# GpSimd instead of ScalarE issues the loads of the staged weights and the stores of their halves

## The reference

```python
h = _layernorm(x, axis=-1) * (1 + ca) + sa
x = x + ga * _L0_attn_ref(h, Wqkv, bqkv, Wout, bout)      # 16 heads, causal softmax
h = _layernorm(x, axis=-1) * (1 + cb) + sb
# feed-forward, E, H, I = (8, 256, 512), TOP_K = 1
logits = x @ router_w.T
top_vals, top_idx = jax.lax.top_k(logits, TOP_K)
...
routed = jnp.einsum('etf,efh->eth', up * jax.nn.silu(gate), down_proj)
shared = jax.nn.silu(x @ shared_gate_w) * (x @ shared_up_w) @ shared_down_w
x = x + gb * (shared + routed_sum)
```

## Time and profile before

| | us |
|---|---|
| median of 3 runs | 463.87 |
| lowest and highest | 460.45, 464.77 |
| the profiled execution | 461.35 |
| its span, first to last instruction | 459.6 |
| busy in it: PE, DVE, ACT, POOL | 398.2, 313.6, 227.7, 212.8 |

### The profile page before, as it was taken

The page is one execution under the profiler, slowest core; times in us unless marked ns, Lnnn a source line. Parts: engine busy times, 40 slices in busy tenths (PEclk is TensorE's granted clock), DMA queues, the critical chain, the costliest instruction groups (busy, mean ns, idle before and its releaser), DMA issues.

```text
span 459.6 us, 8603 instructions
## 1 busy us (share of the span) xinstructions
PE 398.2 (87%) x3009; PEld 224.8 (49%) x3009; DVE 313.6 (68%) x635; ACT 227.7 (50%) x408; POOL 212.8 (46%) x251
## 2 busy tenths in 40 slices
PE   3789986598989899878989799999879999999991
PEld 3244542243554356434435264575555666666660
DVE  7678597268999898799968864879553434444441
ACT  2445556288584867547865746263213333232320
POOL 2395954343336963177354653101601555555342
PEclk9999999699999999999999999999999999999997
DMA  8547489359692578734357004992700444333210
GB/s 270 165 117 159 166 218 230 118 186 276 243 252 83 170 206 265 210 118 138 96 172 232 1 20 166 397 350 77 227 24 25 84 87 82 83 72 82 26 21 0
DMA packets 46192, 67.96 MB, mean 148 GB/s; under 512 B 5380, under 2 KB 33668, under 8 KB 46152
## 3 DMA queue, kind: packets, MB, share of 16 engines
q1 hardware_dynamic: 31064, 36.74, 27.4%
q10 hardware_dynamic: 9936, 22.55, 15.1%
q0 software_dynamic: 5152, 8.14, 9.0%
HBM read 43.14 MB, written 25.18 MB: 149 GB/s over the span
## 4 chain that ended last, share of the span: by engine, by line
PE 51%; DVE 18%; DMA 9%; ACT 7%; issue 5%; SPq 4%; POOL 3%; ACTq 1%; DVEq 0%; POOLq 0%
PE bank L1513 35%; DVE mx L1146 4%; DMA qk_d<-W 4%; DMA ng_d<-negm 4%; PE bank L1669 3%; PE bank L1653 3%; PE bank L1894 2%; SPq L541 2%; DVE rowg L1247 2%; ACT W L896 2%; PE bank L1624 2%; PE bank L1601 1%; DVE W L1247 1%; DVE x_sb L1191 1%; PE bank L1528 1%
## 5 line engine op out<-in xcount | busy, mean ns | idle before, releaser
L896 ACT ACTIVATE W<-bank 128x512 f32<-128x512 f32 (+1 forms) x176 | 93.7, 562 | 61.6 <-PE bank L1653 43.5
L1146 DVE TENSOR_REDUCE mx<-bank 128x1 f32<-128x384 f32 (+3 forms) x176 | 104.9, 632 | 27.4 <-PE bank L1626 24.0
L1513 PE MATMUL bank<-W 128*128 128x256 f16 (+2 forms) x756 | 103.9, 289 | 5.3 <-DVE x_sb L1191 1.7
L1513 PEld LDWEIGHTS bank<-W 128*128 128x128 f16 x756 | 72.7, 99 | 38.1 <-issue 8.5
L768 POOL TENSOR_SCALAR_AFFINE_SELECT W<-W 128x512 f32<-128x512 f32 x64 | 47.8, 748 | 83.9 <-ACT W L896 83.9
L1653 PE MATMUL bank<-W 128*128 128x512 f16 (+3 forms) x256 | 63.3, 304 | 18.9 <-ACT W L896 9.7
L1513 PE MATMUL bank<-W,h2T 128*128 x276 | 67.3, 380 | 2.8 <-DVE W L1262 2.0
L839 POOL DMA_INDIRECT out<-h2T,sidx x23 | 36.3, 1578 | 67.5 <-DVE h2T L1483 67.1
L1624 PE MATMUL bank<-W 126*128 126x128 f16 (+3 forms) x208 | 52.5, 304 | 5.6 <-DVE mx L1146 4.2
L1669 PE MATMUL bank<-W 128*32 128x128 f32 (+3 forms) x512 | 48.6, 454 | 0.8 <-POOL W L768 0.8
L1653 PEld LDWEIGHTS bank<-W 128*128 128x128 f16 x256 | 21.3, 97 | 55.6 <-ACT W L896 29.2
(11 more groups left out here) (173 smaller groups left out, 558.8 us busy)
## 6 DMA issues: line engine op xcount, KB each, us to landing
w_d<-rowg ACTq DMA_DIRECT2D x18, 512.0 KB, 3.7
W<-w_d SPq DMA_DIRECT2D x18, 512.0 KB, 7.9
stage<-in_gup ACTq DMA_DIRECT2D x14, 512.0 KB
qk_d<-W SPq DMA_DIRECT2D x48, 128.0 KB
W<-qk_d SPq DMA_DIRECT2D x32, 192.0 KB, 5.1
stage<-in_down ACTq DMA_DIRECT2D x7, 512.0 KB
x_sb<-in_x SPq DMA_DIRECT2D x4, 512.0 KB, 9.5
h_d<-gbb SPq DMA_DIRECT2D x4, 512.0 KB, 4.6
```

Of the source, the lines that this page charges most:

```text
L896: a.activation(PT[j][:, i:i + m, :], t_bank(N)[:, 0:m * w].rearrange("p (i n) -> p i n", i=m), ACT.Exp).then_inc(s_exp, 1)
L1146: v.tensor_reduce(mx_v[:, b % 2, hp0 // 4, par, i:i + m, t], s_bank(N)[:, 0:m * w].rearrange("p (i n) -> p i n", i=m), AX.X, ALU.max).then ...
L1513: i = t_.matmul(outp, l, r, start=(n == 0), stop=(n == len(prods) - 1), **kw)
```

## The change: what it does

`move_halves` leaves ScalarE's stream and enters GpSimd's, at the end of the same step. GpSimd waits for the low half, issues the store, then the load of unit k + 3. The loads that GpSimd issues count on semaphores of their own (`s_pld`); ScalarE's `split_high` waits for those from unit 3 on.

```diff
@@ -388,6 +388,7 @@
         s_eld = [sem(f"s_eld{r}") for r in range(3)]
+        s_pld = [sem(f"s_pld{r}") for r in range(3)]
@@ -497,7 +498,7 @@
             e, u = unit_list[unit(k)]
-            dst, s = staged(k), s_eld[k % 3]
+            dst, s = staged(k), s_eld[k] if k < 3 else s_pld[k % 3]
@@ -774,6 +775,13 @@
+            def move_halves(k):
+                po.wait_ge(*low_done(k))
+                if k < BOUNCED:
+                    g.dma_start(w_d[k], ob[k % 2]).then_inc(s_bw[k % 2], 16)
+                if k + 3 < NU:
+                    unit_in(g, k + 3)
@@ -814,6 +822,9 @@
+                    moved = splits_at(BU * b + n - MOVES)
+                    if moved is not None:
+                        move_halves(moved)
@@ -933,7 +944,7 @@
             def split_high(k):
-                ac.wait_ge(s_eld[k % 3], 32 * (k // 3 + 1))
+                ac.wait_ge(*((s_eld[k], 32) if k < 3 else (s_pld[k % 3], 32 * (k // 3))))
@@ -944,13 +955,6 @@
-            def move_halves(k):
-                ac.wait_ge(*low_done(k))
-                if k < BOUNCED:
-                    ac.dma_start(w_d[k], ob[k % 2]).then_inc(s_bw[k % 2], 16)
-                if k + 3 < NU:
-                    unit_in(ac, k + 3)
@@ -1019,9 +1023,6 @@
-                    moved = splits_at(BU * b + n - MOVES)
-                    if moved is not None:
-                        move_halves(moved)
```

## The result

| | before | changed |
|---|---|---|
| median, us (executions) | 462.16 (4) | 471.77 (4) |
| lowest and highest | 458.15, 464.77 | 470.07, 472.93 |
| the profiled execution, its span | 461.35, 459.6 | 470.88, 469.1 |

The ratio is 1.0244, 95% interval 1.0198 to 1.0289. The change is slower: by 9.6 us between the medians, by about 11 us by the ratio, and by 9.5 us between the two profiled executions. The forecast was 468.4, range 460.0 to 476.0.

What follows compares the result with a forecast made beforehand. No engine was taken as the bound for long: TensorE, VectorE, ScalarE and GpSimd walk in step through the attention loop. -2.5 + 4.9 + 3.4 = +5.8 us on the mean of 462.6 gave 468.4 us, range 460.0 to 476.0.

Steps and rivals of the forecast that it cites:

- The sum: Whole kernel: ScalarE's gain and GpSimd's two late places give +5.8 us; the moved transfers themselves were priced at 0.
- place 1: Sequence 1, ahead of the last `modulate2`: four transfers of units 10 and 11 make GpSimd late for TensorE, +4.9 us.
- three signs: Wrong if new GpSimd rows short, down units' rows 3 times others, or TensorE's `h2_turn` waits under 2 us both places.
- Part 2: GpSimd's price per transfer, taken from gathers: 1.27 us (range 0.4 to 4.3), 56 us for 44, mostly covered by waits.
- Part 3: Sequence 1, second norm: four transfers at 1.27 us, 5.08 less 0.14 us to spare, cost +4.9 us.
- Part 4: Sequence 2, second norm: three transfers delay `rstd`, two more stand behind the first `modulate2`; TensorE waits, +3.4 us.
- Place 2: Sequence 2, about 200 to 216 us: five transfers make GpSimd's mask and `modulate2` late for TensorE, +3.4 us.
- Part 1: ScalarE's issues on the chain: stops near 171 (0.78 us) and 187 us (1.71) vanish, -2.5 us; near 207 nothing.
- rival 2: Attention loop: engines walk in step and absorb late work, so the end does not move (464.3 or 462.0 us); chance 0.25.
- Rival 1: GpSimd hides issues of under about 0.3 us each and ScalarE is set free: faster, 457.7 us; chance 0.08.
- Rival 3: Down-unit loads of 512 pieces cost GpSimd 4.3 us instead of 1.27, one at each place: 474.5 us; chance 0.17.
- Rival 4: VectorE's norm scalings hold up GpSimd's nine transfers at both places, 0.5 us each, 4.4 us more: 472.8 us; chance 0.08.

Runs made afterwards that it cites:

- 2: Against the kernel before: GpSimd issues the transfers from unit 8 on, ScalarE those of units 0 to 7; ratio 1.0129, median 467.08 us.
- 7: Against the changed kernel: moves of units 3 to 6 one step earlier in GpSimd's stream; ratio to the kernel before 1.0193.
- 9: Against the changed kernel: in sequence 0 moves of units 3 to 6 earlier and ahead of `qk_low`; ratio to the kernel before 1.0115, median 464.94 us.
- 10: Against the kernel before: GpSimd issues the moves from unit 8 on except units 10 and 11, ScalarE the rest; ratio 1.0018.
- 12: Against the changed kernel: units 3 to 6 issued early, ahead of `qk_low`, and ScalarE issues units 10 and 11; ratio to before 1.0010, median 461.78 us.
- 8: Against the kernel before: GpSimd issues only the moves of units 13 and 15, ScalarE the rest; ratio 0.9976, median 459.64 us.

## Why the prediction was right or wrong

**Right:** slower by over 1% had 0.54, and 471.77 lies in the range. **But half of the loss is another one than I named.** The sum had -2.5 + 4.9 + 3.4 = +5.8; the runs show relay +5.9, place 1 +4.8, everything else +0.5. **By two of its own three signs the prediction was wrong:** the new rows are short (0.56 to 0.60 us and back to back, not 0.96 and 0.30 apart), and TensorE's waits for `modulate2` before `h2_turn` are 0.7 us in both places. That the total lies in the range is in part luck, since a term left at nothing and a price twice too high made up for each other.

**The step that failed** is in the sum: "The transfers themselves are the same bytes to the same places, issued 0 to 3 us later ... : 0". I had looked at who waits for the moved transfers (nobody for 6 steps) and not at who shares the DMA engines with them. The earlier trace rows stood first in the argument: TensorE waits 7.8 us for `W<-ng_d`. (That piece ends at 85 us, at the relay one sequence earlier; at the one near 112 us, where the changed kernel waits 7.0, it was 0.2 us before.) A chain that runs over transfers at a DMA share of 0.9 to 1.0 is the one place where a shift of 1 MB by 2 us must be priced. I used those rows only to say that gains ahead of them count for nothing; in the changed kernel a loss there counted in full.

**Part 2, the price of a transfer, was mis-sized:** 1.27 us from the gathers, measured 0.56 to 0.60, and 0.79 for 512 pieces. GpSimd's busy time rose by 27 us (239.6 against 212.8), not by 42. The nearest row was not near: a gather is indirect, and a plain transfer is half its price. With the measured prices Part 3 gives 2.6 - 0.14 = +2.5 us. Part 4 gives 0 ahead of `rstd`, then 0.60 + 0.79 - 0.91 = +0.5 us for the two transfers ahead of the mask, which had 0.91 us of idle time.

**Place 1 was the right place and mechanism.** Predicted +4.9; the profiles show +3.1 to +4.3, the ratios 4.8. The transfers are 2.6 us of it, not 5.1, and the low half that now meets GpSimd ahead of the last `modulate2` is 1.0 us. TensorE's longest wait of 2.3 us is for the stretched mask ahead of it, not for `modulate2`. The sum was near because a price twice too high stood in for a stretch that I had not seen there.

**Place 2 is far smaller than predicted (+3.4):** `rstd` is not late, and GpSimd loses 0.6 us on the two transfers behind it. The exponentials fall back 2.2 us between steps 22 and 38, but they had gained 2.8 just before. Over steps 12 to 38 the net is -0.5 us in kernels 2, 7, 9, 10, 12 and the changed one, and -1.1 us in 8, where GpSimd issues unit 15's move but not unit 16's: 0.6 us for place 2, from profiles alone.

**Part 1:** the stop at 187 us is real, 2.0 us by step 16 in kernels 8, 12 and the changed one (predicted 1.7). The one at 171 us gave nothing (predicted 0.8). In kernel 8 half of the first is given back by step 22, as rival 2 said of engines that walk in step.

**The rivals.** Rival 1 needed about 0.3 us an issue to be faster, and set the point where gain and loss cancel at 0.6. The measured price is at that point, yet the kernel is far slower, since place 1 costs more than the transfers' own time and the relay was in neither. Rival 3 falls: 0.79 us, not 4.3. The Trainium skill, "DMA: Bandwidth & Descriptors" (section "Anatomy of one DMA — SWDGE (gpsimd) path"), which let many descriptors pass before the increment, agrees with that. Rival 4 put the cost on the wrong instructions. The 18 stores take 0.55 to 0.84 us, median 0.58, so the transfers are held up by 0.3 us at most. Of the nine in the two places three lie beside a scaling (0.65, 0.55 and 0.63 us, no longer than elsewhere), and none of the 44 beside a low half, so what that would do to a transfer was not seen. But the mask and the `modulate2` behind them lost 1.0 us to VectorE's low half, once at place 1 and not nine times 0.5. The low half reads two buffers, `stage` and `rowg`, and by the Trainium skill, "SBUF — State Buffer" (section "Who interferes with whom"), a VectorE instruction with two SBUF inputs contends with a GpSimd instruction that reads SBUF. The 1.62 us against 0.63 agree in direction; no run here shows that this is the cause. The row of 1.58 us at 205.77 that the prediction showed also lies beside a low half, the one at 205.27, for 1.0 us, and beside a scaling for only 0.2. The Trainium skill, "DMA: Bandwidth & Descriptors" (section "SWDGE vs HWDGE vs iDMA"), says that the transfer engines round-robin between queues of the two kinds. One could take that to mean that a load of 8 KB passes a backlog of another queue soon; the section gives no time for it. The table shows 1.8 us against 4.8 us, with GpSimd's backlog as with ScalarE's: the measured number decides, and a backlog costs it 3 us.

**What stays open:** whether the stretch beside the low half comes from shared ports (no kernel took the low half away), why the `qk_d` hop is 2 us longer behind a later unit 3 (how its packets stand in the queues was not seen), how often the kernel before loses the race, and why holding unit 6 back alone brings no gain in the median.

## What to carry to other kernels

- Moving the issue of a transfer moves the transfer. List the small transfers on the critical path that run in the same microseconds, and price the shift by their rows, however little the moved transfer itself is waited for.
- An engine that runs its stream in order and has idle time on average still issues late: in 7 a step earlier in the code was 0.1 us earlier on the chip. Read the issue times, then place the issue ahead of the engine's own long instructions, not by step number.
- Where an engine is pushed, see what it will newly stand beside: here, in the profile of place 1, that was 1.0 of 3.6 us.
- If two timings race, one profile shows one outcome. The profile of before had won by 0.4 us; an unchanged sequence 0 in another kernel's profile showed the other side.

## What the runs showed of the hardware

- A plain transfer of 512 KB costs GpSimd 0.56 to 0.60 us of its time, one of 512 pieces 0.79 us, back to back. In the profile of before ScalarE's queue took 0.33 to 0.36 us for a store and mostly 0.35 to 0.48 us for a load, in single cases up to 1.67.
- An 8 KB load took 1.8 to 2.0 us ahead of a 1 MB move on another queue and 4.5 to 5.0 us when it was issued 0.7 us or more behind it (seven profiles). All transfers together ran at 338 GB/s in the first case (before, 111.4 to 113.7 us) and 351 in the second (changed).
- A GpSimd instruction beside VectorE's low half for 1.1 us took 1.0 us longer: mask 1.62 for 0.63, `modulate2` 1.69 for 0.73, `qk_low` 2.14 for 1.15.
- In an idle wait of 7.0 us TensorE's granted clock fell to 0.50 and stayed there for 4 us of work behind it (the same four matmuls 0.43 against 0.23 us). In kernel 9 it stayed at 1.00 after a wait of 1.65 us at 111.7 us, and fell to 0.50 for 3.4 us behind the waits of 2.3 and 0.7 us of place 1. Of the 8.7 us of the relay's step some 2 come from this: the first matmul is 5.7 us later than before, the exponentials 7.5.
